# GNN kernel on one core: the halves of entry groups 3 to 6 made by GpSimd, and group 2's sums taken ahead of the short tile

## The reference

```python
h = maximum(layernorm(x), 0)
h = tanh(h @ W_in + b_in)                       # the entry
for _ in range(12):                             # the steps
    agg = segment_sum(h[src], dst) / deg
    h = h + (tanh(gelu(agg @ W1 + b1) @ W2 + b2) - decay * h) * 0.5
x = x + h
h = maximum(layernorm(x), 0)
x = x + two_gcn_layers(h)                       # same edges, degree-normalised
```

## Time and profile before

| | us |
|---|---|
| median of 3 runs (lowest, highest) | 1315.54 (1315.1, 1318.03) |
| the profiled execution, its own time | 1316.1 |
| its span in the trace | 1314.4 |
| TensorE busy | 1257.7 (96% of the span) |
| VectorE busy | 400.9 (30%) |
| ScalarE busy | 299.5 (23%) |
| GpSimd busy | 44.2 (3%) |
| mean granted TensorE clock | 0.988 of full |

### The profile page before, as it was taken

The page is one execution under the profiler, slowest core; times in us unless marked ns, Lnnn a source line. Parts: engine busy times, 40 slices in busy tenths (PEclk is TensorE's granted clock), DMA queues, the critical chain, the costliest instruction groups (busy, mean ns, idle before and its releaser), DMA issues.

```text
span 1314.4 us, 17281 instructions
## 1 busy us (share of the span) xinstructions
PE 1257.7 (96%) x7194; PEld 709.1 (54%) x7194; DVE 400.9 (30%) x817; ACT 299.5 (23%) x438; POOL 44.2 (3%) x56
## 2 busy tenths in 40 slices
PE   2779899999999999999999999999999999999998
PEld 1666356565564565645645556456455564564545
DVE  6899114022131131221311312113013132482312
ACT  1798213122131121211311212112112131120100
POOL 4800000000000000000000000000000000000000
PEclk8899999999999999999999999999999999999999
DMA  3000200000000000000000000000000000220101
GB/s 98 3 1 1 62 1 1 0 1 0 0 0 0 0 0 0 0 0 0 0 0 0 0 0 0 0 0 0 0 0 0 0 0 17 69 63 0 50 17 34
DMA packets 24552, 13.77 MB, mean 10 GB/s; under 512 B 6173, under 2 KB 23609, under 8 KB 24388
## 3 DMA queue, kind: packets, MB, share of 16 engines
q1 hardware_dynamic: 22334, 11.88, 3.5%
q10 hardware_dynamic: 1782, 1.06, 0.3%
q0 software_dynamic: 400, 0.33, 0.1%
HBM read 9.42 MB, written 3.44 MB: 10 GB/s over the span
## 4 chain that ended last, share of the span: by engine, by line
PE 90%; DVE 6%; DMA 2%; issue 2%; ACT 1%; SPq 0%; DVEq 0%; POOL 0%; ACTq 0%; POOLq 0%
PE ps L701 63%; PE ps L743 10%; PE ps L734 9%; PE ps L639 5%; DVE scratch L1144 3%; PE ps L612 2%; PE ps L807 1%; DMA adj<-adj 1%; DVE lo L1127 1%; DMA adj<-packed_scratch,adj 1%; ACT adj L889 0%; PE ps L569 0%; DVE cols L1343 0%; DMA adj<-in_dst_dram 0%; DVE state L1370 0%
## 5 line engine op out<-in xcount | busy, mean ns | idle before, releaser
L701 PE MATMUL ps<-adj,hi 128*128 128x512 f16 (+2 forms) x2275 | 747.2, 352 | 1.3 <-DVE lo L1127 1.3
L701 PE MATMUL ps<-adj,lo 128*128 128x512 f16 (+2 forms) x2184 | 730.4, 351 | 0.0
L701 PEld LDWEIGHTS ps<-adj,hi 128*128 128x128 f16 x2275 | 220.8, 97 | 228.0 <-issue 14.5
L701 PEld LDWEIGHTS ps<-adj,lo 128*128 128x128 f16 x2184 | 212.4, 97 | 224.1 <-issue 18.2
L1271 DVE TENSOR_TENSOR ps<-ps,bias 128x512 f32<-128x512 f32 (+1 forms) x84 | 53.9, 641 | 535.9 <-PE ps L743 535.9
L931 ACT ACTIVATE scratch<-ps 128x512 f32<-128x512 f32 (+1 forms) x84 | 46.3, 552 | 618.1 <-DVE ps L1271 618.0
L922 ACT ACTIVATE scratch<-ps,b1c,cols 128x512 f32<-128x512 f32 (+2 forms) x168 | 112.0, 724 | 170.7 <-PE ps L734 169.9
L743 PEld LDWEIGHTS ps<-w,scratch 128*128 128x128 f32 x1200 | 144.2, 192 | 8.1
L743 PE MATMUL ps<-w,scratch 128*128 128x128 f32 x1200 | 146.1, 275 | 0.0
L734 PE MATMUL ps<-scratch,w 128*128 128x512 f32 (+2 forms) x336 | 137.8, 538 | 0.0
L1264 DVE TENSOR_TENSOR scratch<-ps,scratch 128x512 f32<-128x512 f32 (+2 forms) x84 | 51.9, 619 | 185.3 <-PE ps L734 139.6
(11 more groups left out here) (143 smaller groups left out, 270.0 us busy)
## 6 DMA issues: line engine op xcount, KB each, us to landing
scratch<-rdeg_scratch SPq DMA_DIRECT2D x1, 1562.5 KB, 10.5
state<-in_x_dram SPq DMA_DIRECT2D x5, 256.0 KB, 4.0
scratch<-in_x_dram SPq DMA_DIRECT2D x5, 256.0 KB, 2.7
x_scratch<-state SPq DMA_DIRECT2D x5, 256.0 KB, 2.8
scratch<-dinv_scratch SPq DMA_DIRECT2D x5, 256.0 KB, 3.7
state<-x_scratch SPq DMA_DIRECT2D x5, 256.0 KB, 3.2
out_dram<-state SPq DMA_DIRECT2D x5, 256.0 KB
adj<-adj ACTq DMA_DIRECT2D x1, 390.6 KB, 9.6
```

The costliest lines, as they stand in the source:

```text
L701: return nc.tensor.matmul(bank, values[:, k, :], adj[:, k, c0:c0 + n], start=is_first, stop=is_last)
```

## The change

Two parts. In the entry, groups 3 to 6 have their `hi` made by GpSimd (a `tensor_scalar` of 128x512, for group 6 of 128x128, behind its row normalisation) instead of ScalarE, and their `lo` is made by VectorE behind the one-hots of batches 23, 27, 31 and 33 instead of 20, 24, 28 and 32. `ENTRY_BATCHES` stays 34 and `EARLY_PARTS` stays as it was. In the first step TensorE takes group 2's 24 full tiles ahead of the wait for `s_pair`; then come the short tile's products of groups 0, 1 and 2, one after the other; `hidden` of group 0 moves in between the first 8 and the last 16 full tiles of group 3. From group 3's short tile on the order is as before. The other lines (in the branches on `missed`) aren't executed with these inputs.

```diff
--- before.py
+++ after.py
@@ -67,7 +67,8 @@
 EVERY = 4
 TURN_AT = [2 + EVERY * g for g in range(NG)]
 PROD_AT = [b + EVERY // 2 for b in TURN_AT]
-LO_AT = [b + 4 for b in PROD_AT]
+POOL_HI = 3
+LO_AT = [b + (4 if g < POOL_HI else 7 if g < TAIL else 5) for g, b in enumerate(PROD_AT)]
 ENTRY_BATCHES = (LO_AT[-1] + 2) // 2 * 2
 EARLY_TILES = 2
 EARLY = EARLY_TILES * (BATCHES - ENTRY_BATCHES)
@@ -530,6 +531,10 @@
                     last = nc.gpsimd.tensor_scalar(state[:, k, :], state[:, k, :], ln_a[:, k:k + 1], ln_b[:, k:k + 1],
                                                    ALU.mult, ALU.add)
                 last.then_inc(s_y, 1)
+            for g in range(POOL_HI, NG):
+                pool.wait_ge(s_upd, g + 1)
+                nc.gpsimd.tensor_scalar(tiles_of(hi, g), tiles_of(state, g), first_scale, None, ALU.mult
+                                        ).then_inc(s_hi, 1)
             pool.wait_ge(s_flag, 1)
             missed = pool.value_load(flag[0:1, 0:1], min_val=0, max_val=1)
             with pool.If(missed != 0):
@@ -653,6 +658,11 @@
 
             with pe.If(missed != 0):
                 pe.wait_ge(s_last[2], 1)
+                for g in range(2):
+                    if EARLY_PARTS[g][1]:
+                        c0, n = SPANS[g]
+                        nc.tensor.matmul(ps[:, FIRST_BANK[g], 0:n], hi[:, 0, :], adj[:, 0, c0:c0 + n],
+                                         start=False, stop=True)
                 pe.wait_ge(g_conv, 1)
 
                 def tile_sum(j, number, left):
@@ -680,7 +690,8 @@
                     tile_sum(j, TILES, lambda s: g_one)
                 pe.wait_ge(g_degk, 5 + OPEN)
                 for g in range(2):
-                    first_sums(g, EARLY_PARTS[g])
+                    if EARLY_PARTS[g][1]:
+                        first_sums(g, EARLY_PARTS[g])
                 pe.wait_ge(g_apair, 16)
 
 
@@ -767,22 +778,30 @@
                 outputs(t, TAIL)
 
             def first_step():
-                if EARLY_PARTS[1][1] < FULL:
-                    first_sums(1, (EARLY_PARTS[1][1], FULL))
-                for g in range(NG):
-                    if g >= 2:
-                        first_sums(g, (0, FULL))
-                    pe.wait_ge(s_pair, 16)
+                def rest_and_short(g):
                     c0, n = SPANS[g]
                     bank = ps[:, FIRST_BANK[g], 0:n]
                     with pe.If(missed != 0):
                         with pe.Fori(0, TILES) as r:
                             add_rest(0, g, bank, r)
                     first_sums(g, (FULL, TILES)).then_inc(s_agg, 1)
-                    if g >= 3:
-                        outputs(0, g - 3)
-                    if g >= 2:
-                        hidden(0, g - 2)
+
+                if EARLY_PARTS[1][1] < FULL:
+                    first_sums(1, (EARLY_PARTS[1][1], FULL))
+                first_sums(2, (0, FULL))
+                pe.wait_ge(s_pair, 16)
+                for g in range(3):
+                    rest_and_short(g)
+                for g in range(3, NG):
+                    if g == 3:
+                        first_sums(g, (0, HEAD))
+                        hidden(0, 0)
+                        first_sums(g, (HEAD, FULL))
+                    else:
+                        first_sums(g, (0, FULL))
+                    rest_and_short(g)
+                    outputs(0, g - 3)
+                    hidden(0, g - 2)
                 edge_sums(1, 0, (s_hi, s_lo), NG, (0, GROUP_TILES))
                 outputs(0, TAIL - 2)
                 hidden(0, TAIL - 1)
@@ -901,7 +920,8 @@
                     entry_copy(TURN_AT.index(b))
                 if b - 1 in PROD_AT:
                     entry_tanh(PROD_AT.index(b - 1))
-                    split_hi(PROD_AT.index(b - 1), PROD_AT.index(b - 1) + 1, first_scale)
+                    if PROD_AT.index(b - 1) < POOL_HI:
+                        split_hi(PROD_AT.index(b - 1), PROD_AT.index(b - 1) + 1, first_scale)
             with act.Fori(ENTRY_BATCHES // 2, BATCHES // 2) as i:
                 for u in range(2):
                     evict(u, i)
```

## The result

Both kernels were run 17 times. The changed kernel has a median of 1313.88 us (1311.33 to 1314.97), the kernel before 1316.2 us (1315.1 to 1318.03). The ratio of the medians is 0.9979, with a 95% interval of 0.9972 to 0.9987: 2.3 us less, or 0.2%, where 5.0 us were forecast. The sign was right and the size was not. (The forecast of 1310.5 us was counted from a median of 1315.54 us over three runs; from 1316.2 it would be 1311.2, so the miss is 2.7 us.) The time lies inside the range that I gave, at its upper edge, but by luck: the range was made from other causes than the one that the runs show. The profiled execution took 1314.08 us, its span is 1312.4 us, 2.0 under the span before.

What follows compares the result with a forecast made beforehand. TensorE was taken as the bound, with VectorE pacing it from 60 to 104 us. Terms -4.74 - 1.70 + 0.2 + 1.2 = -5.0 us, from a median of 1315.54, gave 1310.5 us; range 1308.8 to 1314.0.

Steps and rivals of the forecast that it cites:

- The wait for the pair and the slow clock behind it: First step: TensorE's 4.74 us wait for the short tile's transfer and 1.70 us of slow clock both go, 6.44 us.
- The three branches: First step: three short products in a row, each with a branch ahead, cost 0.2 us in all.
- Late next: First step: the next possible waits, for group 0's means, hidden and gelu, stay covered; gelu's cover is 5 us deep.
- lo later, nothing: Entry: making lo three batches later on VectorE costs zero, if hi is there.
- hi off ScalarE, nothing: Entry: relieving ScalarE gains nothing, since nobody on the path waits for it; at most a 0.2 us wait.
- What GpSimd does to VectorE: Entry: GpSimd takes pieces between VectorE's instructions, 0.37 us for each of three wide hi, 0.09 for group 6: 1.2 us more.
- The lock that holds VectorE for the whole of GpSimd's instruction: Entry rival: VectorE stands for all of GpSimd's undisturbed time, 5.8 us, giving 1315.1 us, no change; chance 9%.
- Even that would not stop VectorE for long: Entry: at up to 10.8 us per hi, two thirds are done at 82.25 us; VectorE waits 0.6 us.
- the signs that I had named for being wrong: VectorE idle before lo until GpSimd ends; one-hots of 2 us; batch 34 past 106; first-step waits; clock under 1 after 104.
- The rule of the Trainium skill that I had set against my sum: Entry: two-input VectorE instructions and GpSimd reads of SBUF fully block each other for a whole instruction; 5.8 us, not 1.2.
- my third rival: Late entry: a slow-clock spell falls where TensorE sets the pace, costing up to 1.7 us; 1311.4 to 1312.2 us; chance 17%.

Runs made afterwards that it cites:

- run 17: Not a follow-up run but a count: the changed kernel and the kernel before were each run 17 times, medians 1313.88 us and 1316.2 us.
- e1: The changed kernel with the entry of before (every hi on ScalarE, old lo places), only the new first step kept: 1310.24 us, ratio 0.9956 to the kernel before.
- e10: The same kernel as e1, timed once more on another occasion: 1309.26 us, ratio 0.9948 to the kernel before.
- e3: The changed kernel with hi of groups 3 to 6 back on ScalarE, the later lo kept: 1309.79 us, ratio 0.9957 to the kernel before.
- e2: The changed kernel with the old order in the first step, GpSimd's hi and the later lo kept: 1320.33 us, ratio 1.0036 to the kernel before.
- e6: e1 plus four GpSimd products of the state into an unused tile, which nobody waits for in the entry: 1311.47 us, ratio 0.9966.
- e4: The changed kernel with lo of groups 3, 4 and 5 later still, at batches 26, 30 and 32: 1313.22 us, ratio 0.9982 to the kernel before.
- e7: As e6, but GpSimd only fills the unused tile and reads no input: 1310.34 us, ratio 0.9956 to the kernel before.
- e5: The changed kernel with a short VectorE fill without inputs behind the one-hots of batches 20, 24 and 28: 1312.3 us, ratio 0.9973 to the kernel before.
- e8: e1 with three more of group 1's full tiles put before TensorE's wait for the last copy, ahead of the branch: 1311.98 us, ratio 0.9963.

## Why the prediction was wrong, step by step

**The wait for the pair and the slow clock behind it, 6.44 us: right.** The trace after has neither. With the 0.2 taken for the branches the forecast was 6.2 us; e1 and e10 measured 5.3 and 7.2 by their medians.

**The three branches, 0.2 us: too much.** Four products that hold the three short ones start at 156.27 and the next at 157.13: 0.215 us each, as without a branch. What the step missed is a pause of TensorE's own: the product at 142.86 starts 1.02 us after the one before it, 0.8 more than usual. With it 6.44 becomes 5.6, which is what the trace gives. In e1 and e10 the idle printed at that place is 0.18 and 0.17 us and in e3 0.46, and their stretch to `outputs` is 29.26, 29.26 and 29.53 us. The new order is not what makes the pause: e2, with the old one, prints 0.32 us there, and e6, with the new one, has none.

**Late next: right.** VectorE's means start at 156.69, `hidden` at 160.38 and `outputs` at 169.24, and TensorE waits for none of them.

**lo later, nothing: right. hi off ScalarE, nothing: not shown.** e3 equals e1 within its interval, which speaks for lo. No run frees ScalarE without burdening GpSimd; VectorE waits for ScalarE neither before nor after, from 60 to 104 us.

**What GpSimd does to VectorE, 1.2 us: right in size.** A wide instruction's piece was put at 0.37 us; e6 has 0.35 to 0.42, and the kernel after has a lo of 1.18 us instead of 0.74 and one one-hot of 1.35 instead of 0.93, 0.86 us in all. The lock that holds VectorE for the whole of GpSimd's instruction did not show: 0.42 us of the 1.5 that hi takes once it is in.

**"Even that would not stop VectorE for long": this step failed.** It said that hi goes on at the pace of line 530, four times as long, so that two thirds are done when lo falls due and 0.6 us is left, and even that 0.6 was not carried into the sum. Line 530's instructions had all ended within 2.7 us, so I read a pace into them. In fact hi of group 3 had done nothing at 82.5, and its whole 1.5 us lay ahead; e4 gave it five more microseconds, and again nothing was done. Two of the signs that I had named for being wrong are there: VectorE idle before lo until GpSimd is done, and batch 34 past 106 us (107.80). There was a second omission. I priced the wait as VectorE's time alone and did not ask what TensorE does meanwhile. It stood 3.35 us, ran at 0.50 of its clock from 87 to 93 us, fell behind VectorE, and made it wait 0.97 us more. In e2 and e4 too TensorE stands behind VectorE's stop, 3.4 and 3.25 us. Together: 1.47 for the wait, 0.44 and 0.42 for two stretches, 0.97 less the 0.2 that was there before: 3.1 us, where the sum had 1.2. The last copy is 3.6 us later; 0.2 of them were there already at lo of group 2 (69.73 against 69.50), and 0.3 is not accounted for.

The sum with the measured terms: -5.6 + 3.6 = -2.0, against -5.0.

**Why does the first hi get nothing and the later ones get in?** This stays open. The rule of the Trainium skill that I had set against my sum, page "SBUF — State Buffer", section "Who interferes with whom", names the pairing rightly: two inputs in SBUF on VectorE against a GpSimd instruction that reads, and not against one that only writes. Here e7 agrees, 0.52 us and no stretch, and so does the GpSimd that is fully blocked in e4: this half of the rule, which I had called borne out and then priced at nothing, is the one that cost. VectorE, for its part, is held for a quarter of GpSimd's instruction and not for the whole. But in the kernel after, hi of group 5 got in after 1.3 us between two one-hots of one batch, with no stop of VectorE:

```profile
93.24 0.75 DVE L1147 SCALAR_TENSOR_TENSOR lo<-state,cols,hi 128x512 f16<-128x512 f32 x1
93.49 2.71 POOL L536 TENSOR_SCALAR hi<-state,cols 128x512 f16<-128x512 f32 x1 [8.00 <-ACT state L904]
```

Openings let it in (e5, three of three). The starts in the traces also fall into two kinds. The 128x512 reads that stayed out (group 3 in the kernel after, e2, e4 and e6, and the three of e5 until their fill) all start 0.18 or 0.19 us ahead of VectorE's next instruction. Those that got in by themselves, in 2.6 to 2.8 us (group 5 in the kernel after and e2, group 4 in e4, groups 4 and 5 in e6), start 0.35 to 0.53 us ahead of it. Nor did the first of e6 need a stop: it passed group 3's lo and got in at group 4's. No run moved the start on purpose, so this is a pattern and not a cause.

**The spread.** e1, with the entry of before, had executions from 1308.68 to 1311.64 us. The slowest is the profiled one, and it shows one reason (windows view, columns as in the earlier trace rows):

```profile
104.00:107.00 3.00, 2.48 (x17) 1.82 (x16) 2.79 (x4) 1.81 (x2) 0.00 (x0) 0.50 0.00 0
108.00:110.00 2.00, 2.00 (x24) 1.52 (x22) 1.73 (x3) 1.41 (x2) 0.00 (x0) 1.00 0.04 8
```

The spell that stood at 95 to 98 us in the kernel before falls here at 104 to 107, where TensorE sets the pace, and the last copy comes at 137.50 instead of 135.62 in e10's profile. That is the mechanism of my third rival, and 1.9 us here, where its full price was put at 1.7. It needs no change of the code. Of the ten executions of e1 and e10 the three slowest (1310.95 to 1311.64 us) are the three with the lowest mean clock, 0.985; the others have 0.987 to 0.990.

## What to carry to other kernels

GpSimd is no free engine beside a VectorE that runs back to back on instructions with two inputs in SBUF: here an instruction of 1.5 us took 8.6 and 13.7 us, and both times it started to get on only when VectorE stopped to wait for it. Before work is moved there, ask when VectorE pauses next, and price a wait by what the bound engine behind it does too, its clock included. The reordering that hides a transfer behind sums already at hand gave what was forecast within the noise (6.2 us forecast, 5.3 and 7.2 measured); the two edits should have been tried apart.

## What the runs showed of the hardware that I had not expected

- A GpSimd instruction that reads SBUF can be kept out while some fourteen one-hots pass: 12 us in e4, with one-hots of undisturbed length beside it; a fill of 0.11 us on VectorE lets it in (e5).
- Getting in costs VectorE 0.35 to 0.44 us for 512 columns and 0.09 to 0.17 for 128, whether the whole instruction takes 2.6 or 13.7 us.
- TensorE has pauses that the profile puts down to nothing, and they differ between near-equal kernels: 2.79 us in e8, where it comes to a branch just as two transfers are issued; in e10, which comes to the branch 0.9 us before the transfers, one of 0.17 us ten products later. The cause is open.
